# Two attention stages of a four-layer transformer: VectorE's loop body halved, and the first stage's row maxima and causal masks joined over two heads

## The chip, the cores and the metric

The kernel runs on one core of one Trainium2 chip. A core has five engines that run their own instruction streams and meet at semaphores: TensorE (PE; its weight loads are shown as PEld), VectorE (DVE), ScalarE (ACT), GpSimd (POOL) and SyncE (SP), which issues the transfers. The metric is the device time of one execution in microseconds (us); times of single instructions are partly in nanoseconds (ns).

## The reference, cut to what matters

Four transformer layers work on 16 items of 256 rows by 128 features. Each layer is a modulated attention and a modulated feed-forward block. The first layer's attention has 16 heads of 64 features:

```python
q = (x @ Wq).reshape(B, N, H, Dh).transpose(0, 2, 1, 3)
s = jnp.einsum('bhid,bhjd->bhij', q * scale, k)
gm = jax.lax.stop_gradient(jnp.max(s, axis=-1, keepdims=True))
causal_mask = jnp.triu(jnp.ones((N, N), bool), 1)
p = jnp.where(causal_mask, 0.0, jnp.exp(s - gm))
out = einsum(p, v) / (jnp.sum(p, axis=-1, keepdims=True) + EPS)
```

The row maximum is taken before the mask. The second layer's attention has 8 heads of 128 features, no mask, and a relative-position term, which is shifted by one place per row:

```python
attn = jnp.einsum('bnqd,bnkd->bnqk', Q + rel_embed_bias, K)
attn_pos = relative_shift(jnp.einsum('bnqd,nkd->bnqk', Q + rel_pos_bias, rel_k))
a = jax.nn.softmax(attn + attn_pos, axis=-1)
out = jnp.einsum('bnqk,bnkd->bnqd', a, V)
```

## The kernel before

The whole network is one program of eight stages, one after another, with all activations on the core. The change touches the first stage (`attention0`) and the third (`attention1`). Both walk over 16 items with eight steps to an item, 128 steps in all. A step of `attention0` is one pair of heads, a step of `attention1` is one head. Within a stage every engine has its own instruction stream, and the streams are software pipelines written out by hand: in step `at` an engine also does pieces of the step ahead (`nx`) and of steps behind (`b1`, `b2`, `b3`). The order within a stream is fixed by the text of `step`, and every hand-over is a wait on a semaphore whose count follows from the step's number.

The streams are produced by `walk(engine, steps per item, unroll, lead, lag, step)`. The steps of the first `unroll` items and of the last `unroll` items are written out; those between are a hardware loop whose body holds `unroll` items. With `unroll` 2 the body is 16 steps and runs 6 times, so its closing branch is taken 5 times. In the loop the counts that are waited for are computed in registers. Each engine has a loop of its own, and only DVE's is touched.

In `attention0` a step runs as follows. PE computes the scores of both heads into `s_ps[0]` and `s_ps[1]` (L637, 12 matmuls, two neighbouring banks of PSUM), then nine matmuls for the next step's values, queries and keys (L123 to L125). DVE meanwhile takes the row maxima of head 0 and then of head 1 from the unmasked scores (L709). PE waits for head 0's maxima and adds the mask to head 0 by two matmuls with an identity (L658, L660, `mask(0)`), does the eight matmuls of the output of the pair before last (L673), waits for head 1's maxima and adds its mask (`mask(1)`), then does L685 (output projection) and the transposes of L476. ACT takes the exponentials of head 0 (L566, L568, each with the sum read out behind it), rounds the next keys (L559), takes the exponentials of head 1, then copies the output and the values. PE's next L637 waits for all exponentials of this step, since it overwrites the scores. DVE, after the maxima, normalises the pair before (L715, L717, L722) and cuts the next queries and keys into two parts (L727).

In `attention1` PE makes a head's scores and position scores, DVE adds a table and hands them to SP (L1374), SP writes them to DRAM and reads them back skewed (`a_shifted`), DVE adds the two and takes the maximum (L1363, L1368), ACT takes the exponentials (L1180), DVE normalises (L1344, L1347), and PE transposes (L1252) and multiplies by the values (L1299).

Of the kernel before, what the change touches and what calls it, by code (L numbers as in the profile page):

```python
# [11 lines left out]
ALU = mybir.AluOpType  # L12
ACT = mybir.ActivationFunctionType
AX_X = mybir.AxisListType.X
# [4 lines left out]
NT = T // P  # L19
# [466 lines left out]
def attention0(nc, d, k):  # L486

    phase, PER = 0, 8
# [4 lines left out]
    with ExitStack() as ctx:  # L494
# [11 lines left out]
        den = sb("den", [P, 2, 2, NT])  # L506
        rec = sb("rec", [P, 2, 2, NT])
        qk_ps = k.banks[0:2]
        s_ps, pT_ps = k.banks[2:4], k.banks[4:6]
        o_ps, v_ps, y_ps = k.banks[6][:, 0:T], k.banks[6][:, T:2 * T], k.banks[7]  # L510
        ht_ps = k.psum.rearrange("p (b c) -> p b c", b=8)[:, 4:6, C:512]
        names = ("chain", "var", "std", "rstd", "xn", "ht_mm", "ht", "ht_rounded", "ht_cut", "W_rounded", "W_cut",
# [12 lines left out]
        with nc.Block() as block:  # L525
# [21 lines left out]
            @block.scalar  # L547
            def _(act):
                std_of_rows(act, n, s["var"], s["std"])
                act.wait_ge(k.weights_in[phase], 16 * weight_pieces(phase))  # L550
                for i in range(6):
                    whole, x, part, scale = piece(i)
                    act.activation(W[:, x, 0, part], whole, ACT.Identity, scale=scale).then_inc(s["W_rounded"], 1)

                def step(at):
                    nx, b1, b2, b3 = at.shift(1), at.shift(-1), at.shift(-2), at.shift(-3)
                    def rounded(nx, i):
                        wait(act, s["qk_mm"], nx, 2, 1 - i)
                        act.copy(qk[:, nx.ring(2), i, 0, :], qk_ps[i][:, 0:T]).then_inc(s["qk_rounded"], 1)  # L559

                    def exps(h):
                        r = at.ring(2)
                        wait(act, s["nmax"], at, 2, 1 - h)
                        wait(act, s["masked"], at, 2, 1 - h)
                        wait(act, s["pT_mm"], at.shift(-4), 2)
                        act.activation(p[:, at.ring(4), h, 0:P], s_ps[h][:, 0:P], ACT.Exp,  # L566
                                       bias=nmax[:, r, h, 0:1], accum_out=sums[:, r, h, 0:1])
                        act.activation(p[:, at.ring(4), h, P:C], s_ps[h][:, T:2 * T], ACT.Exp,  # L568
                                       bias=nmax[:, r, h, 1:2], accum_out=sums[:, r, h, 1:2]).then_inc(s["exp"], 1)

                    if b2.real:
                        wait(act, s["pT_mm"], b2, 2, 1)
                        wait(act, s["o_mm"], b2.shift(-2))
                        act.copy(pT[:, b2.ring(2), 0, :], pT_ps[0][:, 0:C]).then_inc(s["pT0"], 1)
                        wait(act, s["pT_mm"], b2, 2)
                        wait(act, s["o_mm"], b2.shift(-2))
                        act.copy(pT[:, b2.ring(2), 1, :], pT_ps[1][:, 0:C]).then_inc(s["pT1"], 1)
                    ni = at.shift(4)
                    if at.p == 4 and ni.real:
                        wait(act, s["ht_mm"], ni, item=True)  # L580
                        wait(act, s["pT0"], b2)
                        modulated(act, k, phase, ni, ht_ps, n.hT[:, ni.s // PER % 2, :].rearrange("p (t q) -> p t q", t=NT),
                                  s["ht"])
                    if nx.real:
                        wait(act, s["s_mm"], nx.shift(-2))
                        rounded(nx, 0)
                    if at.real:
                        exps(0)
                    if nx.real:
                        rounded(nx, 1)  # L590
                    if at.real:
                        exps(1)
                    if b2.real:
                        wait(act, s["o_mm"], b2)
                        wait(act, s["y_mm"], b2.shift(-2))
                        act.copy(oT[:, b2.ring(2), :], o_ps).then_inc(s["oT"], 1)
                    if nx.real:
                        wait(act, s["v_mm"], nx)
                        wait(act, s["o_mm"], nx.shift(-7 - nx.p % 2))
                        act.copy(v[:, nx.s // 2 % 4, nx.p % 2, :], v_ps).then_inc(s["v"], 1)  # L600
                    if at.p == 4 and ni.real:
                        cut_hT(act, n, ni, s["ht"], s["ht_rounded"])
                    if at.p == 2 and b3.real:
                        take_sum(act, n, b3, y_ps, s["y_mm"], s["biased"], s["taken"])

                walk(act, PER, 2, LEAD, LAG, step)

            @block.tensor
            def _(pe):
# [3 lines left out]
                def step(at):  # L613
# [40 lines left out]
                            matmul3(pe, qk_ps[i][:, 0:T], [W[:, i, part, nx.p * P:(nx.p + 1) * P] for part in range(2)],  # L654
                                    halves(n.hT2, item, 0, T)).then_inc(s["qk_mm"], 1)
                    def mask(h):
                        wait(pe, s["nmax"], at, 2, 1 - h)
                        pe.matmul(s_ps[h][:, 0:P], k.ident_bf[:], k.causal_bf[:], start=False, stop=True,  # L658
                                  skip_group_check=True)
                        pe.matmul(s_ps[h][:, T + P:2 * T], k.ident_bf[:], k.causal_bf[:], start=False, stop=True,  # L660
                                  skip_group_check=True).then_inc(s["masked"], 1)

                    if at.real:
                        mask(0)
                    if b2.real:
                        wait(pe, s["pT0"], b2)
                        wait(pe, s["pT1"], b2)
                        wait(pe, s["v"], b2.shift(1 - b2.p % 2))
                        wait(pe, s["oT"], b2.shift(-1))
                        r, slot, c = b2.ring(2), b2.s // 2 % 4, b2.p % 2 * P  # L670
                        for j in range(NT):
                            for h in range(2):
                                mm = pe.matmul(o_ps[64 * h:64 * h + 64, j * P:T],  # L673
                                               v[:, slot, j, c + 64 * h:c + 64 * h + 64],
                                               pT[:, r, h, 0:T] if j == 0 else pT[:, r, h, T:C],
                                               start=(j == 0), stop=(j == 1), skip_group_check=True)
                        mm.then_inc(s["o_mm"], 1)
                    if at.real:
                        mask(1)
                    if b3.real:  # L680
                        wait(pe, s["oT"], b3)
                        if b3.p == 0:
# [10 lines left out]
            def _(dve):  # L693
# [9 lines left out]
                def step(at):  # L703
                    nx, b1, b2, b3 = at.shift(1), at.shift(-1), at.shift(-2), at.shift(-3)
                    if at.real:
                        for h in range(2):
                            wait(dve, s["s_mm"], at)
                            wait(dve, s["exp"], at.shift(-2), 2)
                            dve.tensor_reduce(nmax[:, at.ring(2), h, :],  # L709
                                              s_ps[h][:].rearrange("p (t k) -> p t k", t=NT), AX_X, ALU.max,  # L710
                                              negate=True).then_inc(s["nmax"], 1)
                    if b1.real:
                        r = b1.ring(2)
                        wait(dve, s["exp"], b1, 2)
                        dve.tensor_scalar(den[:, r], sums[:, r], EPS, None, ALU.add).then_inc(s["den"], 1)  # L715
                        wait(dve, s["den"], b1)
                        dve.reciprocal(rec[:, r], den[:, r]).then_inc(s["rec"], 1)  # L717
                        wait(dve, s["rec"], b1)
                        for h in range(2):
                            for t in range(NT):  # L720
                                c = p[:, b1.ring(4), h, 0:P] if t == 0 else p[:, b1.ring(4), h, P:C]
                                i = dve.tensor_scalar(c, c, rec[:, r, h, t:t + 1], None, ALU.mult)  # L722
                        i.then_inc(s["p"], 1)
                    if nx.real:
                        for i in range(2):
                            wait(dve, s["qk_rounded"], nx, 2, 1 - i)
                            dve.tensor_tensor(qk[:, nx.ring(2), i, 1, :], qk_ps[i][:, 0:T],  # L727
                                              qk[:, nx.ring(2), i, 0, :], ALU.subtract).then_inc(s["qk"], 1)

                    if at.p == 2 and at.shift(6).real:  # L730
                        normalise(dve, n, at.shift(6), s["ht_mm"], s["xn"])
                    if at.p == 3 and at.shift(-4).real:
                        row_stats(dve, n, at.shift(-4), s["added"])

                walk(dve, PER, 2, LEAD, LAG, step)

def prefetch(sp, nc, k, d, phase):
# [289 lines left out]
def attention1(nc, d, k):  # L1028
# [12 lines left out]
    with ExitStack() as ctx:  # L1041
# [46 lines left out]
        with nc.Block() as block:  # L1088
# [218 lines left out]
            def _(dve):  # L1307
# [67 lines left out]
                                                  r_rows[:, n2.p, first:first + PITCH], ALU.add)  # L1375
                        i.then_inc(s["pos"], 1)

                walk(dve, PER, 2, LEAD, LAG, step)

def ffn1(nc, d, k):
# [1219 lines left out]
```

## Time and profile before

| | |
|---|---|
| median of 3 runs | 2787.06 us (2785.50 to 2788.62) |
| the profiled execution | 2791.02 us, of which 2789.3 us are the profile's span |
| PE busy | 2515.3 us, 90% of the span |
| PE weight loads busy | 2068.7 us, 74% |
| DVE busy | 1871.5 us, 67% |
| ACT busy | 1424.9 us, 51% |
| POOL busy | 656.9 us, 24% |
| mean granted clock of TensorE | 0.959 of full speed |
| `attention0` | about 47 to 647 us of the span |
| `attention1` | about 970 to 1497 us of the span |

The shares of busy time are averages over eight stages with different limits. What an edit in one stage is worth has to be read from that stage's own chain of hand-overs. Matmuls overlap in the pipeline, so the busy time of PE counts the stretch that they cover, not work at peak.

### The profile page before, as it was taken

The page shows a single profiled execution, that of the slowest core. Times are in us where ns is not written, and L with a number is a line of the kernel's source. Part 1 is how long each engine was busy: PE and PEld are TensorE (multiplying, and loading weights), DVE is VectorE, ACT ScalarE, POOL GpSimd, SP SyncE. Part 2 cuts the span into 40 slices and gives each one's busy share as a digit, 9 for nine tenths or more (in the row PEclk, how much of TensorE's full clock was granted, in tenths as well). Part 3 has the DMA queues.
Part 4 walks back from the last instruction along what each step waited for, and adds up shares of the span by engine and source line. Part 5 has one row for each costly group of instructions (what it writes and reads, how often), then busy time and mean ns, then how long its engine had stood idle before and what let it go on. Part 6 is the DMA issues. An engine that isn't in the chain of part 4 may idle for free. (4 is left out here: it accounts for less than half of the span.)

```text
span 2789.3 us, 61608 instructions
## 1 busy us (share of the span) xinstructions
PE 2515.3 (90%) x19690; PEld 2068.7 (74%) x19752; DVE 1871.5 (67%) x5884; ACT 1424.9 (51%) x3993; POOL 656.9 (24%) x1179
## 2 busy tenths in 40 slices
PE   4999999997999899999997999958997886999888
PEld 3888888886888698999996888846665474666566
DVE  4777777775677477878876666656775225777587
ACT  3888888885444355555554323214545132545444
POOL 0000000000111000000000101146774025777322
PEclk9999999998999899999998999979998897999899
DMA  5000000002000354555554000046553744655100
GB/s 148 2 2 1 0 0 1 1 1 64 1 1 1 120 157 151 160 161 160 159 160 99 1 1 0 1 147 173 156 149 80 89 48 116 162 153 147 36 14 18
DMA packets 196188, 212.33 MB, mean 76 GB/s; under 512 B 12628, under 2 KB 179940, under 8 KB 194676
## 3 DMA queue, kind: packets, MB, share of 16 engines
q1 hardware_dynamic: 195956, 209.64, 28.3%
q8 instruction: 96, 1.57, 0.3%
q14 instruction: 136, 1.11, 0.1%
HBM read 108.95 MB, written 90.65 MB: 72 GB/s over the span
## 5 line engine op out<-in xcount | busy, mean ns | idle before, releaser
L709 DVE TENSOR_REDUCE a_nmax<-bank 128x2 f32<-128x512 f32 x256 | 165.0, 686 | 155.9 <-PE bank L637 155.9
L1180 ACT ACTIVATE a_p<-a_p,a_nmax 128x256 f32<-128x256 f32 x256 | 128.3, 502 | 227.3 <-DVE a_nmax L1368 227.3
L221 POOL TENSOR_TENSOR delta<-y,arena 128x256 f32<-128x256 f32 x32 | 24.7, 771 | 814.9 <-ACT y L214 814.9
L1823 ACT ACTIVATE a_p<-bank 128x1024 f32<-128x1024 f32 (+1 forms) x256 | 193.5, 808 | 25.2 <-PE bank L1878 21.4
L1450 ACT ACTIVATE f_silu<-bank 128x512 f32<-128x512 f32 x128 | 76.7, 599 | 211.6 <-PE bank L125 210.7
L1766 POOL TENSOR_SCALAR_AFFINE_SELECT a_p<-a_p 128x512 f32<-128x512 f32 x256 | 163.0, 637 | 0.0
L2032 DVE TENSOR_REDUCE a_nmax<-bank 128x4 f32<-128x1024 f32 x128 | 155.6, 1216 | 2.8 <-PE bank L1865 2.8
L902 ACT ACTIVATE f_hidden<-bank,arena 128x512 f32<-128x512 f32 x128 | 87.8, 686 | 126.7 <-PE bank L125 126.7
L1019 DVE SCALAR_TENSOR_TENSOR f_acc<-bank,f_cw,f_acc 128x128 f32<-128x128 f32 x448 | 125.5, 344 | 37.8 <-PE bank L965 37.0
L965 PEld LDWEIGHTS bank<-arena,f_hidden 128*128 128x128 f32 x1024 | 133.8, 191 | 19.3 <-DVE f_acc L1019 3.6
L965 PE MATMUL bank<-arena,f_hidden 128*128 128x128 f32 x1024 | 142.7, 278 | 3.7 <-DVE f_acc L1019 3.0
L559 ACT CAST a_qk<-bank 128x256 fp32r<-128x256 f32 x256 | 95.1, 371 | 96.8 <-PE bank L125 96.8
L1531 DVE TENSOR_TENSOR f_hidden<-f_silu,bank 128x512 f32<-128x512 f32 x128 | 87.7, 685 | 84.0 <-PE bank L125 62.6
L1299 PE MATMUL bank<-a_v,a_pT 128*128 128x128 f32 x1024 | 138.3, 279 | 4.4 <-ACT a_pT L1163 4.4
L1504 PEld LDWEIGHTS bank<-arena,f_hidden 128*128 128x128 f32 x1024 | 132.9, 191 | 10.3
L722 DVE TENSOR_SCALAR a_p<-a_p,a_rec 128x128 f32<-128x128 f32 (+1 forms) x512 | 135.3, 328 | 4.5
L1299 PEld LDWEIGHTS bank<-a_v,a_pT 128*128 128x128 f32 x1024 | 132.5, 194 | 7.0 <-ACT a_pT L1163 5.9
L1504 PE MATMUL bank<-arena,f_hidden 128*128 128x128 f32 x1024 | 135.3, 275 | 0.0
L1374 DVE TENSOR_TENSOR a_pos<-bank,arena 128x384 f32<-128x384 f32 x256 | 130.7, 552 | 4.4 <-PE bank L125 2.8
L637 PE MATMUL bank<-a_qk 64*128 64x256 f32 x1536 | 126.5, 295 | 6.7 <-ACT a_p L568 3.8
L637 PEld LDWEIGHTS bank<-a_qk 64*128 64x128 f32 x1536 | 103.2, 187 | 32.3 <-DVE a_qk L727 30.1
L568 ACT ACTIVATE a_p<-bank,a_nmax 128x256 f32<-128x256 f32 x256 | 121.9, 476 | 0.0
(328 smaller groups left out, 7736.8 us busy)
## 6 DMA issues: line engine op xcount, KB each, us to landing
pos_dram<-a_pos SPq DMA_DIRECT2D x128, 383.0 KB, 2.8
a_stack<-rows_dram SPq DMA_DIRECT2D x128, 320.0 KB, 4.1
rows_dram<-a_cut SPq DMA_DIRECT2D x192, 192.0 KB, 2.4
a_shifted<-pos_dram SPq DMA_DIRECT2D x128, 256.0 KB, 2.7
f_merged<-f_staged SPq DMA_DIRECT2D x16, 578.0 KB, 9.0
gate<-gates_dram SPq DMA_DIRECT2D x32, 256.0 KB, 11.4
arena<-in_task SPq DMA_DIRECT2D x4, 1156.0 KB, 8.5
x<-in_x SPq DMA_DIRECT2D x4, 512.0 KB, 8.3
```

The costliest lines, as they stand in the source:

```text
L637: mm = pe.matmul(s_ps[h][:, t * T:(t + 1) * T], qk[64 * h:64 * h + 64, at.ring(2), 0, a, t * P:(t + 1) * P], qk[64 * h:64 * h + 64, at.rin ...
L709: dve.tensor_reduce(nmax[:, at.ring(2), h, :], s_ps[h][:].rearrange("p (t k) -> p t k", t=NT), AX_X, ALU.max, negate=True).then_inc(s["nma ...
L722: i = dve.tensor_scalar(c, c, rec[:, r, h, t:t + 1], None, ALU.mult)
L965: mm = pe.matmul(y, hidden[:, at.ring(2), t * P:(t + 1) * P], w["e2w"][:, at.p, :], start=(t == 0), stop=not last, skip_group_check=True)
L1019: i = dve.scalar_tensor_tensor(out=a, in0=z, scalar=c[:, t, at.p:at.p + 1], in1=a, op0=ALU.mult, op1=ALU.add)
L1180: i = act.activation(p[:, at.ring(4), t, :], p[:, at.ring(4), t, :], ACT.Exp, bias=nmax[:, r, t:t + 1], accum_out=sums[:, r, t:t + 1])
L1299: mm = pe.matmul(y[:, t * P:(t + 1) * P], pT[:, b2.ring(2), j, t * P:(t + 1) * P], v[:, slot, j, h * P:(h + 1) * P], start=(b2.p == 0 and ...
L1374: i = dve.tensor_tensor(pos[:, n2.ring(2), t, :], pos_ps[t][:, 0:PITCH], r_rows[:, n2.p, first:first + PITCH], ALU.add)
L1504: mm = pe.matmul(y_ps[e % 2][:, t * P:(t + 1) * P], hidden[:, at.ring(2), t * P:(t + 1) * P], w["w3"][:, e, c, :], start=(c == 0 and t == ...
L1766: pool.affine_select(blocks, blocks, [[0, 4], [1, P]], ALU.is_ge, 0.0, base=0, channel_multiplier=-1).then_inc(s["causal"], 1)
L1823: act.activation(p[:, b4.ring(2), first:end], sT_ps[:, first:end], ACT.Exp).then_inc(s["exp"], 1)
L2032: dve.tensor_reduce(nmax[:, half, 1, of], s_ps[:, 2 * T:6 * T].rearrange("p (c q) -> p c q", c=4), AX_X, ALU.max, negate=True).then_inc(s[ ...
```

## The change

In both stages DVE's stream is unrolled over one item instead of two. Its loop body is then 8 steps, runs 14 times, and its closing branch is taken 13 times; the steps of items 1 and 14, which had been written out, move into the loop.

In `attention0` the row maxima of both heads are taken by one instruction over the two neighbouring banks, and `nmax` is counted once for a step instead of twice. PE adds both masks directly behind one another, ahead of the output matmuls. ACT waits for the joint maxima before either head's exponentials, and still for each head's own mask.

```diff
@@ attention0, setup
-        s_ps, pT_ps = k.banks[2:4], k.banks[4:6]
+        s_ps, pT_ps, both_s = k.banks[2:4], k.banks[4:6], k.psum[:, 2 * 512:4 * 512]
@@ attention0, ACT, exps(h)
-                        wait(act, s["nmax"], at, 2, 1 - h)
+                        wait(act, s["nmax"], at)
@@ attention0, PE
                     def mask(h):
-                        wait(pe, s["nmax"], at, 2, 1 - h)
+                        wait(pe, s["nmax"], at)
...
                     if at.real:
                         mask(0)
+                        mask(1)
...
                         mm.then_inc(s["o_mm"], 1)
-                    if at.real:
-                        mask(1)
@@ attention0, DVE
-                        for h in range(2):
-                            wait(dve, s["s_mm"], at)
-                            wait(dve, s["exp"], at.shift(-2), 2)
-                            dve.tensor_reduce(nmax[:, at.ring(2), h, :],
-                                              s_ps[h][:].rearrange("p (t k) -> p t k", t=NT), AX_X, ALU.max,
-                                              negate=True).then_inc(s["nmax"], 1)
+                        wait(dve, s["s_mm"], at)
+                        wait(dve, s["exp"], at.shift(-2), 2)
+                        dve.tensor_reduce(nmax[:, at.ring(2)].rearrange("p h t -> p (h t)"),
+                                          both_s.rearrange("p (g k) -> p g k", g=2 * NT), AX_X, ALU.max,
+                                          negate=True).then_inc(s["nmax"], 1)
...
-                walk(dve, PER, 2, LEAD, LAG, step)
+                walk(dve, PER, 1, LEAD, LAG, step)
@@ attention1, DVE
-                walk(dve, PER, 2, LEAD, LAG, step)
+                walk(dve, PER, 1, LEAD, LAG, step)
```

## Rows read from the trace of the kernel before

**Rows 1.** Busy time of each engine over a stretch of each attention stage.
```profile
core 0: us, PE busy (x) PEld busy (x) DVE busy (x) ACT busy (x) POOL busy (x), PEclk, DMA share, GB/s
60.00:620.00 560.00, 553.80 (x5189) 452.72 (x5189) 406.47 (x1259) 455.78 (x1730) 41.72 (x57) 1.00 0.00 1
970.00:1497.00 527.00, 499.61 (x3616) 476.41 (x3616) 417.54 (x1580) 295.70 (x869) 45.27 (x60) 0.99 0.51 158
```

**Rows 2.** Timeline of one step of `attention0`: start, us, what, idle before it.
```profile
209.86 0.80 PEld L637 LDWEIGHTS bank<-a_qk 64*128 64x128 f32 x12 [0.32 <-DVE a_qk L727]
209.89 0.97 PE L637 MATMUL bank<-a_qk 64*128 64x256 f32 x12
...
210.90 1.29 DVE L709 TENSOR_REDUCE a_nmax<-bank 128x2 f32<-128x512 f32 x2 [1.39 <-PE bank L637]
...
211.96 0.10 PEld L658 LDWEIGHTS bank<-causal_bf,ident_bf 128*128 128x128 bf16 x1
...
212.34 0.37 ACT L566 ACTIVATE a_p<-bank,a_nmax 128x128 f32<-128x128 f32 x1 [0.16 <-PE bank L660]
212.51 1.01 DVE L722 TENSOR_SCALAR a_p<-a_p,a_rec 128x128 f32<-128x128 f32 x4
...
213.05 0.22 PE L660 MATMUL bank<-causal_bf,ident_bf 128*128 128x128 bf16 x1
...
213.15 0.37 ACT L559 CAST a_qk<-bank 128x256 fp32r<-128x256 f32 x1
213.40 0.39 ACT L566 ACTIVATE a_p<-bank,a_nmax 128x128 f32<-128x128 f32 x1
213.44 0.75 DVE L727 TENSOR_TENSOR a_qk<-bank,a_qk 128x256 fp32r<-128x256 f32 x2
...
213.58 0.64 PEld L476 LDWEIGHTS bank<-ident,a_p 128*128 128x128 f32 x6
...
214.11 0.22 ACT L568 ACTIVATION_READ_ACCUMULATOR a_p<-bank,a_nmax 128x1 f32 x1
...
214.44 0.80 PEld L637 LDWEIGHTS bank<-a_qk 64*128 64x128 f32 x12 [0.23 <-DVE a_qk L727]
```

**Rows 3.** Instructions that write or read `a_nmax`: count, ns min/median/max.
```profile
L709 DVE TENSOR_REDUCE a_nmax<-bank x256: 679/686/693, 49.0 to 644.8; 128x2 f32<-128x512 f32 x128
L2032 DVE TENSOR_REDUCE a_nmax<-bank x128: 1206/1215/1226, 1861.9 to 2601.8; 128x4 f32<-128x1024 f32 x128
```

**Rows 4.** Waits, 60 to 620 us: us in total, times, longest.
```profile
DVE a_nmax L709 <- PE bank L637: 144.6, 120, 1.6
ACT a_pT L574 <- issue: 7.5, 5, 1.6
```

**Rows 5.** Timeline of `attention0` where the loops of DVE and ACT restart.
```profile
200.21 0.98 PE L637 MATMUL bank<-a_qk 64*128 64x256 f32 x12
201.35 1.29 DVE L709 TENSOR_REDUCE a_nmax<-bank 128x2 f32<-128x512 f32 x2 [1.50 <-PE bank L637]
```

**Rows 6.** Waits, 970 to 1497 us (`attention1`).
```profile
DVE spare L74 <- DMA a_shifted<-pos_dram: 24.3, 41, 3.0
...
DVE a_rec L1344 <- issue: 16.9, 5, 3.7
```

**Rows 7.** DMA queues in 11 us around one restart of DVE's loop in `attention1`.
```profile
q14 instruction: 4, 0.03, 1.1%
```

**Rows 8.** Timeline of PE in `attention1` behind that restart.
```profile
1171.60 0.66 PE L1252 MATMUL bank<-ident,a_p 128*128 128x128 f32 x4 [1.78 <-DVE a_p L1347]
```

**Rows 9.** Busy time in `attention1`, 14 us each, around restarts and mid-body item borders in turn.
```profile
1164.00:1178.00 14.00, 11.62 (x85) 10.92 (x84) 9.13 (x38) 6.28 (x21) 0.00 (x0) 1.00 0.44 136
...
1196.00:1210.00 14.00, 13.74 (x100) 13.10 (x99) 11.46 (x44) 8.65 (x26) 0.29 (x1) 1.00 0.52 153
...
1229.50:1243.50 14.00, 12.04 (x78) 11.25 (x77) 9.17 (x38) 6.37 (x21) 0.00 (x0) 0.88 0.44 136
...
1261.00:1275.00 14.00, 14.00 (x109) 13.74 (x108) 11.81 (x47) 8.63 (x26) 0.00 (x0) 1.00 0.50 151
```

## The prediction

> **What bounds the kernel now.** I read the busy times of the two stages first, then a timeline of one step of `attention0`, then the waits of each stage, then the places where DVE's loop restarts.
>
> In `attention0` PE is busy 553.80 of 560 us and DVE 406 [rows 1]. That looks like a stage bound by PE alone, with DVE free. The timeline says more [rows 2]. A step lasts 4.58 us, from one L637 weight load at 209.86 to the next at 214.44. The last L637 load is held back: PE sat idle 0.23 us before it. The row names DVE's L727 as releaser, but that pair ended at 213.44 + 0.75 = 214.19, while ACT's last sum readout ended at 214.11 + 0.22 = 214.33, 0.11 us ahead of the load. L637 overwrites the scores, so it needs ACT's exponentials; ACT is what it waits for. Followed back, ACT runs without a gap from 212.34 (head 0's exponentials, the rounding at 213.15, head 1's exponentials from 213.40), and what let it start at 212.34 was the first mask, whose load stood at 211.96. The cycle of a step is therefore: L637 and the nine matmuls on PE, first mask, ACT's stretch, next L637. DVE's maxima are a side branch that reaches the first mask. The pair starts at 210.90; one of them takes 0.686 us [rows 3], so head 0's maxima were there at 211.59, and PE came for them at 211.96. The side branch has 0.37 us less the hand-over to spare.
>
> In `attention1` PE is busy 499.61 of 527 us [rows 1], so about 27 us are open. Five times DVE sits idle before L1344 with nothing that the profile can name, 16.9 us in all, 3.38 us each [rows 6]; five is how often the loop's branch is taken. In 11 us around one such place four packets of instruction code are loaded [rows 7], so the wait is for code. Behind it PE waits 1.78 us for DVE's `a_p` [rows 8]. In `attention0` no such wait stands in DVE's rows; there it is ACT that restarts late, 5 times, 7.5 us in all [rows 4].
>
> **The joint maxima.** Two reductions of 128x512 go, one of 128x1024 comes. The same form is in the trace elsewhere: 1206 to 1226 ns, mean 1.216 us [rows 3]. The pair took 1.29 us [rows 2], so DVE gains 0.07 us a step and both maxima exist at start + 1.216 instead of start + 0.69 and start + 1.29. For head 0 that is 0.53 us later. The hand-over from DVE to PE is read where PE waits for DVE: L722 ends at 212.51 + 1.01 = 213.52, L476 loads at 213.58, so 0.06 us. The first mask can now load at 210.90 + 1.216 + 0.06 = 212.18 instead of 211.96, **0.22 us later** (0.216 unrounded from the durations; by the shortest and longest instruction 0.21 to 0.23). The 0.37 us of slack is used up and 0.22 is left over.
>
> Behind the first mask on PE stand its second mask, L673, L685 and L476; behind it on ACT stand both heads' exponentials, the rounding and the copies. ACT's stretch has no gap to give back: it starts and ends 0.22 us later, and so does the next L637. Period 4.58 + 0.22 = 4.80 us. DVE's own 0.07 us lies beside this: it makes `a_p` ready earlier for L476, whose transposes end ahead of L637's wait anyhow.
>
> **The second mask.** It moves ahead of L673. Its result existed at 213.05 + 0.22 = 213.27 and ACT came to head 1 at 213.40, after the rounding L559. An earlier mask brings ACT nothing, since ACT is in order. PE's work stays the same four matmuls; a change of shape between them may cost or save up to 0.1 us a step, which the 0.23 us of idle before L637 covers in ordinary steps. If that cover were gone it would add 0.1 x 128 = 13 us; I take nothing.
>
> **How many steps.** There are 128 (256 reductions in rows 3, two a step). The first two fill the pipeline. In the five where ACT restarts late, by 1.5 us against its usual wait, the delay is covered. That leaves 121 x 0.216 = 26.1 us. At a restart DVE's reduction starts later too: 201.35 - 200.21 = 1.14 us after L637 [rows 5] against 210.90 - 209.89 = 1.01 [rows 2]. That 0.13 us was inside the slack and now counts. Of 14 loop heads about 6 coincide with ACT's late ones or their like, so 8 x 0.13 = 1.0 us. Sum for `attention0`: **+27 us**. From below 115 x 0.21 = 24, from above 128 x 0.25 = 32.
>
> **DVE's shorter loop.** In `attention0` DVE has no late restart to lose. In `attention1` the body halves. I expect it to stay loaded, so that the 5 late restarts go and the 13 short ones cost little. Worth is read from PE, not from DVE's 16.9 us. In 14 us around a restart PE is busy 11.62 and 12.04 us; in 14 us around the item border in the middle of a body, 13.74 and 14.00 [rows 9]. The difference is 13.87 - 11.83 = 2.04 us. PE made up the rest of the 3.38 us from work that had piled up. 5 x 2.04 = **-10 us**. The waits for `a_shifted`, 24.3 us over 41 times [rows 6], are late next: the round trip through DRAM starts from L1374 on DVE and won't shorten. From below the gain is 5 us (if each of the 13 restarts costs 0.4 us of its own), from above 17 us (DVE's whole idle time).
>
> The Trainium skill, "Runtime: NRT & Kernel Launch", section "Instruction fetch mechanics", says that an engine other than PE holds 32 KiB of instructions, that code is fetched ahead only in sequence, and that a taken branch to code outside the window waits for a transfer. By that alone more taken branches could mean more waits, 13 in place of 5, which would be against this change. The rows show both outcomes, a wait in the one stage and none in the other, for bodies of 16 steps each; no run here shows a body of 8.
>
> **Sum.** +27 - 10 = +17 us. The durations are from the profiled execution, 2791.02 us with its 2789.3 us of span, which would become 2808. It stands 4 us above the median of the runs, 2787.06; on the median the forecast is **2804 us**, 0.6% slower. What a measurement of this kernel can tell from no change is about 0.2%, or 5.6 us.
>
> **The rivals.**
> - *PE's wait is absorbed, the loop alone counts* (faster). If ACT's stretch were not the binding one, or the joint reduction were ready within 1.0 us, `attention0` would stay and 10 us come off: 2777. It decides where reduction plus hand-over falls below 1.06 us. Against it: 1206 ns is the shortest of 128. Chance 0.05; the case that half is absorbed (2790) 0.04.
> - *`attention1` gives back everything DVE waited.* +27 - 17: 2797. For it: 27 us of PE's idle time are there. Against it: in mid-body PE is already busy 98 to 100%. Chance 0.10.
> - *`attention1` gives nothing*, because the transfers or the restarts of the other engines hold the same place: +27, 2814. Against it: PE's wait is put down to DVE's `a_p`. Shifted code might also make a later loop of DVE restart late, some 2 us more. Chance 0.10.
> - *The short body restarts late too* (the page's rule above taken alone). `attention1`: 13 x 2.04 instead of 5 x 2.04, +16; `attention0`: 13 times the 3.38 us less the 1.39 us that DVE idles there anyway, +26. 2787 + 27 + 16 + 26 = 2856. For it: the wait exists. Against it: a body twice as long restarts in `attention0` without one. Chance 0.05.
> - The forecast has the rest, 0.66.
>
> **How the numbers follow.** The terms' bounds give +24 - 17 = +7 to +32 - 5 = +27, so 2794 to 2814. That takes in the second and third rival and leaves out the first and the fourth, 0.14. Faster by over 0.2% is the first rival alone, 0.05; with half absorbed 2790 is within 0.2%, together with some of the second rival 0.07; slower has 0.88.
>
> **What the changed kernel's profile would show.** The joint reduction at about 1.22 us, 128 times. A wait of PE's L658 for DVE's `a_nmax` of some 0.2 us in nearly every step. Steps of 4.80 us in `attention0`, which then lasts about 27 us longer. ACT's wait for PE before L566 gone up by the same 0.2 us, its stretch to the last readout still 1.99 us. In `attention1` no wait for nothing before L1344, PE busy above 13.5 of 14 us at every item border, the stage about 10 us shorter. The prediction is wrong if the wait at L658 is absent, if the period grows by other than 0.2 us, or if DVE's 13 restarts idle.

## The result, and the profile after

The changed kernel takes 2794.54 us in the median of its runs (2784.83 to 2803.02), the kernel before, run beside it, 2788.22 us (2784.57 to 2794.24). The ratio is 1.0024 with a 95% interval of 1.0015 to 1.0034; the medians stand 6.3 us apart, and the changed kernel is the slower one. Forecast were 2804 us and a range of 2794 to 2814. The direction was right, but the loss is 6 us where 17 were expected. That the median lies inside the range, at its lower edge, is luck: the range stands for a loss of 7 to 27 us over 2787.06 us, and the kernel before measured 1.2 us more beside the changed one. The profiled execution took 2794.39 us, of which 2792.7 are the span.

The joint reduction is as forecast. These are the rows of the tile `a_nmax` in the changed kernel, which answer to [rows 3]; the second row marks first and last step of `attention1`:

```profile
L707 DVE TENSOR_REDUCE a_nmax<-bank x128: 1223/1225/1226, 48.7 to 667.8; 128x4 f32<-128x1024 f32 x128
...
L1366 DVE TENSOR_SCALAR a_nmax<-a_top x128: 168/170/593, 995.7 to 1497.4; 128x2 f32<-128x2 f32 x128
```

The row of the kernel before that the second one answers to:

```profile
L1368 DVE TENSOR_SCALAR a_nmax<-a_top x128: 168/170/589, 969.8 to 1495.9; 128x2 f32<-128x2 f32 x128
```

So `attention0` became longer and `attention1` shorter by nearly the same. From the first group of weight loads of L637 to the last, `attention0` went from 595.8 to 619.8 us, +24.0. `attention1`, from first to last of the row above, went from 526.1 to 501.7 us, -24.4. Between the two stages 2.3 us came in (`attention1` starts 25.9 us later) and behind them 1.9; in the second feed-forward stage (`ffn1`, the one behind `attention1`) DVE's loop restarts late in the changed kernel, which it did not before.

One step of `attention0` in the changed kernel, timeline (start, us, what, idle before), for [rows 2]:

```profile
211.14 0.80 PEld L637 LDWEIGHTS bank<-a_qk 64*128 64x128 f32 x12 [0.28 <-issue]
...
212.18 1.23 DVE L707 TENSOR_REDUCE a_nmax<-bank 128x4 f32<-128x1024 f32 x1 [1.51 <-PE bank L637]
...
213.46 0.10 PEld L658 LDWEIGHTS bank<-causal_bf,ident_bf 128*128 128x128 bf16 x1 [0.26 <-DVE a_nmax L707]
...
213.92 0.37 ACT L566 ACTIVATE a_p<-bank,a_nmax 128x128 f32<-128x128 f32 x1 [0.46 <-PE bank L660]
...
215.69 0.22 ACT L568 ACTIVATION_READ_ACCUMULATOR a_p<-bank,a_nmax 128x1 f32 x1
...
216.03 0.45 PEld L637 LDWEIGHTS bank<-a_qk 64*128 64x128 f32 x6 [0.31 <-issue]
```

The first mask loads 213.46 - 212.18 = 1.28 us after the reduction's start, as worked out ahead (1.216 + 0.06). It is now late: PE sits idle 0.26 us before it, put down to DVE's `a_nmax`. ACT's stretch is what it was, 215.69 + 0.22 - 213.92 = 1.99 us, and ends 0.12 us ahead of the next L637. This step lasts 4.89 us; most last 4.81, where most lasted 4.58 before. The waits from 60 to 660 us, for [rows 4], have the same in the sum:

```profile
DVE a_nmax L707 <- PE bank L637: 171.4, 124, 1.6
...
ACT a_p L566 <- PE bank L660: 45.6, 119, 0.6
PEld bank L658 <- DVE a_nmax L707: 35.0, 124, 0.4
...
ACT a_pT L574 <- issue: 6.1, 5, 1.3
```

The L658 row did not exist before. PE waits 0.28 us in each of 124 steps, and ACT waits 45.6 / 119 = 0.38 us before L566. In the kernel before, from 60 to 620 us, this row was:

```profile
ACT a_p L566 <- PE bank L660: 14.7, 90, 0.2
```

That is 0.16 us each, so ACT waits 0.22 us longer, the amount by which the mask is late.

In `attention1` the wait for nothing is gone. Waits from 980 to 1500 us, for [rows 6]:

```profile
DVE a_rec L1342 <- ACT a_p L1178: 28.0, 113, 1.2
DVE spare L74 <- DMA a_shifted<-pos_dram: 25.0, 60, 2.5
```

There is no row of L1342 with "issue" (time in which the engine waits for nothing that the profile names). The waits for `a_shifted` stayed (24.3 before, 25.0 now). Busy time of the engines, for [rows 1] and [rows 9]: first a long stretch of each stage, then 14 us around four of the 13 places where the loop now takes its branch:

```profile
60.00:620.00 560.00, 547.05 (x4988) 435.57 (x4987) 391.45 (x1095) 438.52 (x1661) 41.64 (x57) 1.00 0.00 1
1000.00:1500.00 500.00, 489.84 (x3602) 470.52 (x3601) 416.86 (x1569) 294.15 (x866) 45.39 (x60) 1.00 0.52 165
1087.00:1101.00 14.00, 12.08 (x91) 11.47 (x91) 10.52 (x40) 6.71 (x20) 1.33 (x2) 1.00 0.49 149
1118.00:1132.00 14.00, 14.00 (x107) 13.58 (x106) 11.95 (x47) 8.13 (x25) 0.00 (x0) 1.00 0.51 161
1149.00:1163.00 14.00, 14.00 (x108) 13.74 (x107) 12.02 (x47) 8.18 (x25) 0.00 (x0) 1.00 0.53 164
1180.00:1194.00 14.00, 14.00 (x107) 13.62 (x107) 11.89 (x47) 8.09 (x25) 0.00 (x0) 1.00 0.52 163
```

PE has no idle time at the last three of these borders. The first of the four is below the 13.5 us that the forecast named as a sign; there DVE waits 3.1 us for the transfer of `a_shifted`, while its branch is followed by the loop's first instruction as fast as at the others. In `attention0` the trap of the busy share shows: PE is still busy 547.05 of 560 us, with 4,988 matmuls begun where it was 5,189, 4% fewer.

### The profile page after: what moved, and what is told of

The parts are those of the page before. It is cut to its first block and busy times, and to the rows that moved or that the text cites. A ratio compares the mean times of both kernels' runs of the same rounds, so it can differ in the third digit from the quotient of the medians.

```text
span 2792.7 us, 61610 instructions
## 1 busy us (share of the span) xinstructions
PE 2528.0 (91%) x19752; PEld 2065.8 (74%) x19752; DVE 1872.3 (67%) x5756; ACT 1424.5 (51%) x3993; POOL 658.7 (24%) x1179
## 5 line engine op out<-in xcount | busy, mean ns | idle before, releaser
L707 DVE TENSOR_REDUCE a_nmax<-bank 128x4 f32<-128x1024 f32 x128 | 156.8, 1225 | 178.3 <-PE bank L637 178.3
L221 POOL TENSOR_TENSOR delta<-y,arena 128x256 f32<-128x256 f32 x32 | 24.7, 773 | 811.1 <-ACT y L214 811.1
L2030 DVE TENSOR_REDUCE a_nmax<-bank 128x4 f32<-128x1024 f32 x128 | 155.6, 1215 | 3.1 <-PE bank L1863 2.9
L637 PE MATMUL bank<-a_qk 64*128 64x256 f32 x1536 | 126.4, 295 | 7.7 <-ACT a_p L568 4.3
L637 PEld LDWEIGHTS bank<-a_qk 64*128 64x128 f32 x1536 | 103.1, 187 | 33.5 <-issue 24.2
```

What stands on the lines that cost most here:

```text
L637: mm = pe.matmul(s_ps[h][:, t * T:(t + 1) * T], qk[64 * h:64 * h + 64, at.ring(2), 0, a, t * P:(t + 1) * P], qk[64 * h:64 * h + 64, at.rin ...
L707: dve.tensor_reduce(nmax[:, at.ring(2)].rearrange("p h t -> p (h t)"), both_s.rearrange("p (g k) -> p g k", g=2 * NT), AX_X, ALU.max, nega ...
L2030: dve.tensor_reduce(nmax[:, half, 1, of], s_ps[:, 2 * T:6 * T].rearrange("p (c q) -> p c q", c=4), AX_X, ALU.max, negate=True).then_inc(s[ ...
```

## The experiments

Twelve more kernels were run, in three groups of four on different chips, each group with the kernel before beside it. Stage times are from each kernel's profile, measured as above. "Late" counts how often DVE's loop in `attention1` sat idle over 2 us at its taken branch; the way into a loop is not counted.

| kernel | `attention0` | `attention1` | late | median | before beside it | ratio (95%) |
|---|---|---|---|---|---|---|
| before | 595.8 | 526.1 | 5 | | | |
| changed | 619.8 | 501.7 | 0 | 2794.54 | 2788.22 | 1.0024 (1.0015 to 1.0034) |
| a1_loop1 | 598.1 | 507.3 | 0 | 2772.93 | 2786.03 | 0.9950 (0.9934 to 0.9965) |
| a0_all | 621.0 | 523.3 | 5 | 2811.41 | 2786.03 | 1.0085 (1.0068 to 1.0102) |
| a0_joint_maxima | 620.1 | 505.8 | 0 | 2794.14 | 2786.03 | 1.0025 (1.0015 to 1.0035) |
| a0_masks_together | 603.4 | 523.3 | 5 | 2793.91 | 2786.03 | 1.0025 (1.0014 to 1.0035) |
| a1_slot0 | 596.1 | 503.4 | 0 | 2770.11 | 2785.04 | 0.9950 (0.9935 to 0.9965) |
| a1_slot109 | 595.9 | 504.5 | 0 | 2766.87 | 2785.04 | 0.9939 (0.9924 to 0.9955) |
| a0_loop1 | 596.9 | 503.5 | 0 | 2769.77 | 2785.04 | 0.9944 (0.9928 to 0.9959) |
| best_slots | 597.5 | 504.6 | 0 | 2770.51 | 2785.04 | 0.9946 (0.9932 to 0.9960) |
| a1_slot111 | 595.5 | 519.3 | 5 | 2781.88 | 2784.07 | 0.9993 (0.9979 to 1.0008) |
| a1_loop4 | 595.6 | 509.6 | 1 | 2771.62 | 2784.07 | 0.9947 (0.9927 to 0.9967) |
| both_loops | 596.9 | 504.6 | 0 | 2769.69 | 2784.07 | 0.9938 (0.9919 to 0.9957) |
| changed_again | 619.6 | 502.8 | 0 | 2794.18 | 2784.07 | 1.0031 (1.0018 to 1.0044) |

The theory at the start: the joint maxima make `attention0` some 24 us longer, the short loop takes away late restarts in `attention1` and these are worth more than 10 us. The rival: the 24 us of `attention1` have another origin (a start later by 26 us, another rhythm of the transfers), so that they would not come from DVE's loop alone.

### The change taken apart

**a1_loop1**: `attention1`'s loop alone.

```diff
@@ attention1, DVE
-                walk(dve, PER, 2, LEAD, LAG, step)
+                walk(dve, PER, 1, LEAD, LAG, step)
```

> Only attention1's DVE loop is unrolled over one item; attention0 is as before. Theory A (the five late restarts cost attention1 some 3.5 us each, and their after-effects the rest): the stage is 22 to 25 us shorter, 2788 becomes 2763 to 2767, and no wait for nothing is left before L1344. Theory B (my forecast's term, a late restart is worth 2.0 us on PE): 10 us shorter, 2778. Theory C (the shorter stage in the changed kernel comes from the other edits or from variation of the transfers): less than 8 us.

Measured 13.1 us faster, `attention1` 18.8 us shorter at 507.3 us, without a late restart. That is less than theory A named and more than theory B's 10 us. The shorter loop is enough to take the late restarts away; neither the later start nor another edit is needed. In this kernel `ffn1`'s loop restarts late, as in the changed one.

**a0_all**: everything in `attention0` (joint maxima, both masks together, its loop over one item), `attention1` untouched.

> attention0 fully as in the changed kernel (joint maxima, masks side by side, loop over one item), attention1 as before. All theories: attention0 24 us longer, the whole 2788 + 24 = 2812. If the two stages add up, this excess and the gain of the run with attention1's loop alone must sum to the +6 us of the changed kernel: with theory A +24 to +28 here. Under 18 us would mean that the stages are not independent.

Measured 25.4 us slower, `attention0` at 621.0 us. `attention1` keeps its five late restarts, here in the waits of 990 to 1525 us:

```profile
DVE a_rec L1342 <- issue: 13.0, 5, 2.8
```

The two parts add up to 25.4 - 13.1 = +12.3 us; the whole measured +6.3 and, run again (changed_again), +10.1. `attention1` went from 526.1 to 507.3 in the one and to 501.7 and 502.8 in the others, which is most of the difference.

**a0_joint_maxima**: the joint reduction without the other two edits of `attention0`.

```diff
@@ attention0, DVE
-                        for h in range(2):
-                            wait(dve, s["s_mm"], at)
-                            ...
+                        wait(dve, s["s_mm"], at)
+                        wait(dve, s["exp"], at.shift(-2), 2)
+                        dve.tensor_reduce(nmax[:, at.ring(2)].rearrange("p h t -> p (h t)"),
+                                          both_s.rearrange("p (g k) -> p g k", g=2 * NT), AX_X, ALU.max,
+                                          negate=True).then_inc(s["nmax"], 1)
```

> Only the maxima are joint; the masks stay apart (head 1's behind L673), DVE's loop over two items. Theory A (head 0's mask waits for the longer reduction, and ACT's stretch behind it moves on the whole): +22 to +26 us, steps of 4.80 us. Rival (PE's order of the masks carries the loss, through the switch of shapes): +5 us or less.

`attention0` did as expected, 620.1 us; its waits from 60 to 620 us show the mechanism as in the changed kernel:

```profile
ACT a_p L566 <- PE bank L660: 41.6, 110, 0.5
PEld bank L658 <- DVE a_nmax L708: 31.5, 115, 0.4
```

But the whole cost 8.1 us only. `attention1`, whose text was not touched, fell from 526.1 to 505.8 us: none of its five restarts was late. So the expected 22 to 26 us for the whole was a miss. The edit shortened DVE's code in `attention0` (a loop body of 235 instructions in the trace where it was 267), and everything behind it moved in the program.

**a0_masks_together**: the second mask directly behind the first, separate maxima.

```diff
@@ attention0, PE
                     if at.real:
                         mask(0)
+                        mask(1)
...
-                    if at.real:
-                        mask(1)
```

> Only the masks stand side by side; the maxima are two instructions. PE then waits for head 1's maxima, at the reductions' start + 1.29 + 0.05 us, before L673, but head 0's mask and with it ACT's stretch start as before. Theory A (what counts is when ACT can start): the wait of about 0.2 us on PE is taken from its idle time before L637, 0 to +4 us in all. Rival (any wait of PE at the masks lengthens the step): +20 to +30 us.

Measured 7.9 us slower, with `attention0` at 603.4 us, +7.6. That is neither theory A's 0 to 4 us nor the rival's 20 to 30. The order of PE's work alone, which the forecast took as nothing, has a price when it stands alone. Timeline of one step:

```profile
206.66 0.80 PEld L637 LDWEIGHTS bank<-a_qk 64*128 64x128 f32 x12 [0.18 <-issue]
...
208.75 0.10 PEld L658 LDWEIGHTS bank<-causal_bf,ident_bf 128*128 128x128 bf16 x1
...
209.04 0.10 PEld L658 LDWEIGHTS bank<-causal_bf,ident_bf 128*128 128x128 bf16 x1 [0.17 <-DVE a_nmax L708]
...
210.06 0.52 PEld L684 LDWEIGHTS bank<-arena,a_oT 128*128 128x128 f32 x4 [0.17 <-issue]
...
210.50 0.69 PEld L476 LDWEIGHTS bank<-ident,a_p 128*128 128x128 f32 x6
...
211.36 0.77 PEld L637 LDWEIGHTS bank<-a_qk 64*128 64x128 f32 x12 [0.17 <-issue]
```

PE comes to the second mask 0.29 us after the first, is held 0.17 us for head 1's maxima, and the step lasts 211.36 - 206.66 = 4.70 us against 4.58. From the L476 load to the next L637 load it is 0.86 us here and 214.44 - 213.58 = 0.86 us before [rows 2]. If the 0.23 us of idle time before L637 had been spare, as the forecast had it, this distance would have shrunk when PE was held earlier. It did not. Medians over the steps from 89 to 609 us say why. L637 loads 0.11 us after ACT's last readout in the kernel before, in the changed one and in a0_joint_maxima, but 0.24 us after it here; from the first L476 load to L637 it is 0.86 us before and here, 0.91 in the changed kernel and 0.95 in a0_joint_maxima. In the kernel before, PE's own chain ends together with ACT's; here PE's ends last, with the joint maxima ACT's.

### What makes a restart late

```profile
q14 instruction: 110, 0.90, 0.1%
```

```diff
-def walk(eng, per, unroll, lead, lag, step, items=NB):
+def walk(eng, per, unroll, lead, lag, step, items=NB, slot=None):
...
-    with eng.Fori(1, items // unroll - 1) as lap:
+    loop = (eng.Fori(1, items // unroll - 1) if slot is None else
+            eng.bass.Fori(1, items // unroll - 1, engines=[eng.engine], head_slot={eng.engine: slot}))
+    with loop as lap:
...
@@ attention1, DVE
-                walk(dve, PER, 2, LEAD, LAG, step)
+                walk(dve, PER, 2, LEAD, LAG, step, slot=109)
```

**a1_slot0**, with `slot=0`, and **a1_slot109**, as above:

> The kernel before, with one thing changed: the head of attention1's DVE loop (still two items, 274 instructions) is placed at slot 0 of a block of instruction memory; no work changes. Theory A (a late restart is a matter of where the body lies): no wait for nothing before L1344, attention1 17 to 22 us shorter, the whole 2766 to 2770. Rival (the length of the body, 16 steps, makes the restart late): as before, 2786.

> As the run at slot 0, but the head at slot 109, so that the body of 274 instructions ends at slot 383, one short of the third border of 128. Theory A: the five late restarts are there as in the kernel before, 2783 to 2790. Rival (any placed head helps, by being on its own): 2766 to 2770.

Neither has a late restart, and both gain what the shorter loop gains: -14.9 and -18.2 us. For a1_slot109 this is the opposite of what theory A said, and what its rival said (any placed head helps); a1_slot111 below decides between them. In both kernels the loop is entered by a jump, and that entry is late once, 2.8 us from branch to loop. a1_slot109 has the lowest median of the study.

**a0_loop1**: DVE's loop over one item in `attention0` alone, as in the change.

> Only attention0's DVE loop over one item; maxima and masks as before. In attention0 itself all theories expect nothing (DVE had no late restart and 0.3 us to spare), 0 to 1 us. The code behind it moves, so theory A allows attention1 either with its five late restarts (2786) or without (2767), and its profile's row for L1344 must say which; a stage that is short with late restarts, or long without, would speak against theory A.

`attention0` 596.9 us, +1.1: the short loop costs next to nothing there. The kernel is 15.3 us faster all the same, since `attention1`'s untouched loop moved and restarted in time, 503.5 us.

**best_slots**: `attention1`'s loop over one item and laid on a border, `ffn1`'s loop laid on a border too (`slot=0` in both).

> attention0 as before; attention1's DVE loop over one item with its head at slot 0; ffn1's DVE loop (355 instructions) at slot 0, so that it fits three blocks of 128. Theory A: attention1 20 us shorter, and ffn1 without the late restart that the code's move gave it in the run with attention1's loop alone (some 2 us): 2764 to 2769, against 2773 there. Rival (ffn1's restart costs nothing): 2773 as there.

14.5 us faster, `attention1` 504.6 us: no better than a1_slot109 or the short loop alone, and between the forecast (2764 to 2769) and its rival (2773). The placed loop of `ffn1` restarts in time, but its entry is late, 2.9 us, so this kernel does not show the gain. The other profiles do: from first to last `f_acc`, `ffn1` lasts 296.3 us in the five kernels where its loop restarts in time and 297.2 to 298.2 in the eight others. One late restart of `ffn1` costs 1 to 2 us.

**a1_slot111**: two instructions further than a1_slot109, and nothing else.

> The kernel before with attention1's DVE loop head at slot 111, two slots on from the run at 109: the body of 274 now ends at slot 385 and touches a fourth block of 128. Theory A: the five late restarts are back, attention1 near 583 us from one clearing of semaphores to the next instead of 563, the whole 2783 to 2790. Rival (a loop placed on purpose doesn't restart late wherever it lies): 2767 to 2770.

Tile `a_nmax`, a1_slot109:

```profile
L1370 DVE TENSOR_SCALAR a_nmax<-a_top x128: 169/170/592, 969.1 to 1473.7; 128x2 f32<-128x2 f32 x128
```

The same row and the waits of 960 to 1500 us, a1_slot111:

```profile
L1370 DVE TENSOR_SCALAR a_nmax<-a_top x128: 168/170/587, 969.5 to 1488.8; 128x2 f32<-128x2 f32 x128
...
DVE a_rec L1346 <- issue: 23.1, 6, 4.7
```

Two instructions of displacement brought all five late restarts back (a sixth wait is at the loop's entry) and made the stage 14.8 us longer. The medians stand 15.0 us apart, on different chips; against the kernel before beside each, the one gains 18.2 us and the other 2.2, just outside the expected 2783 to 2790. In 11 us around one of its restarts three packets of code are loaded:

```profile
q14 instruction: 3, 0.02, 0.7%
```

In a1_slot109 a window of 11 us around a restart has no such queue at all. Length of the body and work are the same in both, so both rivals fall, and so does "any placed head helps".

The kernels whose loops nobody placed settle the rest. Every trace records DVE's instructions with their branches, so the place of each loop can be counted from the first recorded instruction, each loop body taken once. `attention1`'s body of 274 starts at 1840 in the kernel before and in a0_masks_together, at 1463 in a0_all (all late), at 1746 in a0_joint_maxima and at 1509 in a0_loop1 (both in time). Within blocks of 128 that is 48, 48 and 55 against 82 and 101. How far the first recorded instruction lies behind a border is not known, but one distance, 63 to 71 instructions, makes all 78 loops of the fourteen traces right whose place no slot moved, 25 of them late: those whose body touches a fourth block. `ffn1`'s body of 355, in time in the kernel before and late in the changed one, is among them. Blocks of 256 instructions of which two are held would get at least 9 of the 78 wrong, the length alone at least 5.

**a1_loop4**: `attention1`'s body over four items, which the branch closes once.

```diff
-                walk(dve, PER, 2, LEAD, LAG, step)
+                walk(dve, PER, 4, LEAD, LAG, step)
```

> attention1's DVE loop over four items (a body of about 550 instructions, more than four blocks of 128), attention0 as before. It runs twice, so one restart is late instead of five. Theory A at 4 us a restart: four are saved, 16 us, 2769 to 2772. At my forecast's 2 us each: 8 us, 2778.

One late restart, `attention1` 509.6 us, against 504.2 in the mean without any: 5.4 us for one, though the kernels without any range from 501.7 to 507.3. A body that can't fit three blocks is late whenever its branch is taken; it is only taken less often. The same holds for the first feed-forward stage (`ffn0`), whose body of 387 instructions is late in all fourteen traces, 2.8 to 3.1 us from branch to loop.

### What the joint maxima cost in place

**both_loops** has both short loops, without joint maxima and masks together; **changed_again** is the changed kernel beside it on the same chip.

> The changed kernel without the joint maxima and without the moved masks: both stages' DVE loops over one item. Theory A: attention0 as before, attention1 20 us shorter, 2765 to 2771; against the changed kernel in the same call 24 us less, which is what the joint maxima cost. Rival (the loop over one item has a part in attention0's loss): less than 18 us between the two.

> The changed kernel once more, on the same chip as the three others: 2792 to 2796 by every theory, and a second profile to tell how much of the 6 us between the stages' sum and the whole is variation.

2769.69 and 2794.18 us: 24.5 us between them, of which 22.7 stand in `attention0` (619.6 against 596.9). `attention1` differs by 1.8 us the other way. The 3.6 us left over are in no stage: the two profiled executions are 20.4 us apart (2770.35 and 2790.79), which the two stages' 20.9 account for, and that of changed_again ran 3.4 us below its median.

## Why the prediction was right in direction and wrong in size

**`attention0`, +27 forecast, +24.0 measured.** The chain was read rightly: the joint result is late for head 0's mask (1.28 us from the reduction's start, as worked out), the mask is late by 0.22, ACT's stretch is unchanged and passes it on, the step grows from 4.58 to 4.81. Two terms in it were too large or wrongly argued, and that they nearly gave the measured figure is in part luck.
- The sum let 121 steps grow by 0.216 us each. Of the 127 intervals from one L637 group to the next, 102 grew by 0.1 us or more, by 0.234 in the mean, 23.8 us in all. The other 25 together grew by 0.2 us. They are one in the fill, one at the item border where the loops are entered, ten at and just ahead of ACT's late restarts, and 13 of the longer steps (most 5.00 or 5.07 us before, 5.01 or 5.07 after). Why the longer steps absorb the delay was not tried.
- The step that took the masks' move as nothing was wrong as an argument, "which the 0.23 us of idle before L637 covers". Alone the move costs 7.6 us. In the changed kernel it costs nothing visible (620.1 us in a0_joint_maxima, 621.0 in a0_all, 619.8 in the changed kernel): both masks then wait for the same late reduction, and PE's chain no longer ends last. The number was right, the cover was not there.

**`attention1`, -10 forecast, -24.4 measured in this pair of profiles.** Over all kernels, the four with five late restarts have 523.0 us in the mean, the nine with none 504.2: 18.8 us, or 3.8 a restart; in the cleanest pair, slot 111 against 109, it is 3.0. The step that failed is the one behind "The difference is 13.87 - 11.83 = 2.04 us. PE made up the rest of the 3.38 us from work that had piled up." The term of 10 us was too small by half, and PE made up nothing: over the whole stage it lost more than DVE waited at its branch. Two things hid it. The windows between items 1 and 14 show them, of before:

```profile
1004.18:1463.55 459.37, 439.52 (x3194) 420.80 (x3193) 367.13 (x1389) 260.24 (x763) 42.29 (x56) 0.99 0.51 159
```

and of the changed kernel:

```profile
1027.74:1465.61 437.87, 433.15 (x3194) 417.21 (x3193) 369.88 (x1388) 259.83 (x763) 42.40 (x56) 1.00 0.53 166
```

The same 3,194 matmuls are in both. Before, PE was idle 459.37 - 439.52 = 19.9 us, now 4.7; and the same matmuls were "busy" for 439.52 us, now 433.15. So 15.1 of the 21.5 us were idle time, of which two windows of 14 us catch only the part that falls inside them, and 6.4 us were busy time, which is longer when matmuls are held up. TensorE's clock has little part in it: the stretch before holds 6.8 us at the lower of its two levels (granted clock 0.5) and the one after none, but a1_slot109, also with 6.8 us at the lower level and with no late restart, is busy for 434.54 us there, and a1_slot0, with none, for 434.20. And of the mid-body borders taken as undisturbed [rows 9] one has 13.74 of 14 us, where three of the four borders shown above have 14.00; that is a small part.

The upper bound, "17 us (DVE's whole idle time)", fell too. The 16.9 us of [rows 6] are one of four rows in which DVE of the kernel before waits for nothing that the profile names. The other three:

```profile
DVE spare L74 <- issue: 6.4, 6, 2.3
DVE a_p L1363 <- issue: 2.9, 6, 1.1
DVE a_pos L1374 <- issue: 1.6, 6, 0.3
```

All that is left of the four in the changed kernel:

```profile
DVE spare L74 <- issue: 1.8, 3, 0.8
DVE a_p L1361 <- issue: 1.3, 2, 0.7
```

That is 27.8 us before and 3.1 after, a difference of 24.7 us, close to what the stage gave back. What the waits away from the branch are was not followed; that they are late code too is not shown.

The pair of profiles also flatters the change. Five restarts are worth 18.8 us by the means above, and the other 5.6 of the 24.4 us are variation between profiles: of each kind the kernel before has the longest stage and the changed kernel the shortest.

**The rivals.** Of those on record, "`attention1` gives back everything DVE waited" (2797, chance 0.10) is what happened, and more. The late restarts of a later loop, named there as "some 2 us more", did show up in `ffn1`, which lasts 1.1 us longer. That is part of the 1.9 us that came in behind `attention1`. The 2.3 us between the two stages are not of that kind, since `ffn0`'s loop restarts late before and after alike, and their cause is open. None of the 4.2 us was in a term of the forecast. The short body did not restart late, and in `attention0` only the steps named above absorbed the delay.

**The sum as measured:** +24.0 - 24.4 + 4.2 = +3.8 us between the stages of the two profiles, whose spans differ by 3.4; +6.3 between the medians.

## What to carry to other kernels

A stall that recurs at a loop's branch is worth what the stage loses, not what a window around it shows: compare the time of the whole stage over a fixed number of instructions, since busy time stretches too. Before an edit is judged by its time, look whether the same loops restart late in both kernels; an edit of a few instructions elsewhere can switch that on or off and outweigh its own effect. Joining two reductions so that one result comes later is a loss where the first result is on the ring of hand-overs, even when it takes work from an engine with time to spare.

The version that beats both kernels keeps `attention0` as it was and lays DVE's loop in `attention1` where it fits three blocks (a1_slot109, 2766.87 us, 0.6% faster). The short loops without the joint maxima (both_loops, 2769.69) are as good: the ratios are 0.9939 and 0.9938.

## What the runs showed of the hardware

- A loop body of 274 instructions on DVE restarts without a wait at slot 109 (0.3 us from branch to loop) and late at slot 111 (4.1 to 5.2 us); three packets of 8,192 bytes are loaded in 11 us around such a restart.
- The wait belongs to the placement of code that no edit touched: `attention1` lost or kept its five late restarts by an edit in `attention0` (lost in a0_loop1 and a0_joint_maxima, kept in a0_all and a0_masks_together), worth 19 us in the mean over all kernels.
- In 78 loops of fourteen traces DVE's loop restarts late exactly where its body touches a fourth block of 128 instructions, if the first recorded instruction lies 63 to 71 behind a border. Entering a placed loop of two items was late all four times, 2.8 to 3.1 us.
- The same 3,194 matmuls were busy for 439.5 us in a stage with late restarts and 433.2 us in one without.
- A reduction of 128x1024 takes 1.225 us, where two of 128x512 ended 1.29 us after the first one's start: joining them saves 0.07 us and delays the first half's result by 0.54.
